# Weight pieces in two tiles that swap roles, and a queue that takes them step by step

## Chip, cores and metric

One core of a Trainium2 chip. The metric is the device time of one execution in microseconds (us); before the change it is 2639.64 us, the median of three runs (2638.79 to 2642.09).

## What is computed

One adaLN transformer block in float32: four batches of 512 tokens of width 1024; attention with 32 query heads in 8 groups that share a key and a value head, a causal window of 256 tokens; then eight LoRA experts. Cut to what matters here:

```python
q = rope(h @ wq); k = rope(h @ wk); v = h @ wv        # h: modulated layer norm of x
attn = softmax(where(allowed, q @ k.T * 128 ** -0.5, min))
out = (attn @ v).reshape(B, S, 4096) @ wo             # the wo product is the one concerned
x = x + ga * out
x = x + gb * lora_experts(h2)                         # h2: second layer norm
```

## The kernel before

**Numbers.** Every float32 operand of a matmul is split into a hi part (rounded to float32r) and a lo part (what is left); one product is three matmuls, hi by hi, lo by hi, hi by lo (`mm3`, lines 1123 to 1126).

**Groups.** The attention part runs over 32 groups n = 0 to 31: batch n // 8, head group n % 8. For each group TensorE projects K, Q0 to Q3 and V, runs 16 score tiles through softmax and the value product (`pe_attention`, steps u = 0 to 15), and multiplies by the group's 512 rows of wo (`pe_wo`, eight halves: four of them at the steps u = 8, 10, 12, 15, four behind the attention). In TensorE's order group n is: attention of n - 1 with the K projection of n inside it (`K_AT`; in the last group of a batch later, `K_LAST`, from step 5), the four last wo halves of n - 1, Q0 to Q3 of n, V of n.

**Batches.** Batch 0 loads the raw weights, splits them and stores the parts in DRAM (`w_d`). Batch 1 (groups 8 to 15) fetches the split parts. Batches 2 and 3 multiply by wo in a paired form with seven products for eight (`ORDER`, `OUTS`); five of its seven right sides (`MIXED`) are sums and differences of blocks of wo.

**Pieces.** These five are made on GpSimd during batch 1, in 28 pieces (`pool_mix`, line 1007). The queue (SyncE) loads two raw tiles (`sp_mix_load`, 751), GpSimd writes five sums to `mix_lo`, rounds them to `mix_hi` and puts sums less `mix_hi` into `mix_lo`; the queue stores both to `w_s` (`sp_mix_store`, 759). Before a piece GpSimd waits until both stores of the piece before have landed:

```python
            eng.wait_ge(s_raw, WS_KEPT + 32 * piece + 32)
            eng.wait_ge(s_mixd, WS_KEPT + 32 * piece)
```

`MIX_AT` (767) says which pieces belong to which group: 3 each in groups 8 to 12, 4 in 13 and 14, 2 in 15 and 3 in 16. GpSimd makes them behind its masked copies of the probabilities of the attention (`pool_fold`, line 1119) and ahead of the difference of values that the next attention needs (`pool_vd`, 1100).

**The queue's order** is written by hand and is strict: an instruction that waits holds all behind it. For a group of batch 1 (`sp_groups`, 779): the x tile and the turned x tile for the layer norm ahead (groups 9 to 12, `sp_turned_load`, 575; VectorE takes its statistics from the first at steps 11, 13 and 15 of the attention, line 1903), the Q and V weights (`sp_fetch_qv`, once V of the group before is done), K (`sp_fetch_ko`), then what `beside` says, then the wo weights once the group before has done its wo halves (`s_wo`, line 612), then the pieces that are left. `beside` holds the row of rstd and shift for the turned tile (`sp_turned_row`, 580; groups 9 to 12), up to three pieces, and the stores of the tile's two parts (`sp_tile_store`, 589). Behind group 15 `sp_reload` (627) loads hT of batch 2, which the K projection of group 16 reads during the attention of 15; then `sp_enter` (693) begins the paired stage, behind the last pieces.

Of the kernel before, what the change touches and what calls it, by code (L numbers as in the profile page):

```python
# [132 lines left out]
def adaln_block(nc, x, x_turned, wq, wk, wv, wo, gate_wT, lora_aT, lora_bT, c, wmod, cos, sin, mask, keep, lower, ident, iota, out):  # L133
# [12 lines left out]
    with ExitStack() as top:  # L146
# [631 lines left out]

        def sp_groups(eng, b, rows, store):
            if b < PAIRED:  # L780
                for g in range(1, KV):
# [3 lines left out]
                    def beside():
                        if g <= QT:
                            sp_turned_row(eng, b, t)
                        sp_mix(eng, g, range(2))
                        if g <= QT:
                            sp_tile_store(eng, b, t)  # L790
                        sp_mix(eng, g, range(2, min(3, MIX_AT[g + 1] - MIX_AT[g])))
# [2 lines left out]
                    sp_direct_group(eng, n, b, beside)
                    sp_mix(eng, g, range(3, MIX_AT[g + 1] - MIX_AT[g]))
                return
            if b == PAIRED:
                eng.wait_ge(s_mixd, WS_KEPT + 32 * PIECES * (KV - 1))
# [35 lines left out]
        def p1_sp(eng):  # L834
# [25 lines left out]

            def beside():
                sp_mix(eng, 0, range(2))
            sp_fetch_ko(eng, KV, 1, beside)
            sp_mix(eng, 0, range(2, 3))
# [1719 lines left out]
```

## Time and profile before

| | before |
|---|---|
| median of three runs | 2639.64 us |
| the profiled execution | 2638.18 us |
| its span | 2636.3 us |
| TensorE busy | 2520.9 us, 96% |
| VectorE, ScalarE, GpSimd busy | 67%, 44%, 39% |
| mean granted TensorE clock | 0.984 |
| chain that ended last | TensorE 72%, GpSimd 9%, DMA 8%, issue 4%, the queue 3% |

The span is what the profiler records from first to last instruction; the execution's own time is 1.9 us longer. A view of waits says which engine's instruction idled, for what, how often and how long. In a timeline, a bracket at the end of a row is the idle time ahead of it and what ended it. For a DMA a timeline shows when it was issued and how long the issue took, not when it landed.

### The profile page before, as it was taken

What the parts mean: (1) busy time and instruction counts of PE and PEld (TensorE: products, weight loads), DVE (VectorE), ACT (ScalarE), POOL (GpSimd) and SP (SyncE); (2) the same over time, 40 slices, a digit from 0 to 9 for tenths busy, and PEclk for the clock granted to TensorE, in tenths of its full rate; (3) what the DMA queues carried; (4) which work ended last, traced back from release to release, by engine and by line L of the source; (5) the groups of instructions that cost most, each with busy time, mean ns of one, the idle gap of its engine ahead of it and who ended that gap; (6) DMA issues with size and microseconds to landing.
All of it is one profiled execution on the core that took longest, in us unless ns stands there. A gap on an engine that the chain in (4) does not pass through costs nothing.

```text
span 2636.3 us, 42413 instructions
## 1 busy us (share of the span) xinstructions
PE 2520.9 (96%) x12281; PEld 2078.1 (79%) x12281; DVE 1773.3 (67%) x4798; ACT 1169.9 (44%) x2781; POOL 1023.8 (39%) x1278
## 2 busy tenths in 40 slices
PE   7999999999888988889989999999999999999999
PEld 4888888888666776777868888888888888887887
DVE  7677776667565655555677777777777777776653
ACT  4556654453243433333335555443444444445441
POOL 0332332334644544564464444331244443331122
PEclk9999999999899999999999999999999999999999
DMA  8766666676767566656687776666777777767321
GB/s 342 279 230 223 239 241 237 239 257 253 250 239 244 158 219 221 243 184 254 240 259 226 221 230 223 207 207 240 262 248 248 254 239 239 256 227 270 115 81 56
DMA packets 332543, 599.64 MB, mean 227 GB/s; under 512 B 20688, under 2 KB 211984, under 8 KB 330896
## 3 DMA queue, kind: packets, MB, share of 16 engines
q1 hardware_dynamic: 327968, 582.08, 63.3%
q10 hardware_dynamic: 4464, 16.25, 1.6%
q8 instruction: 48, 0.79, 0.1%
q14 instruction: 63, 0.52, 0.1%
HBM read 439.89 MB, written 158.38 MB: 227 GB/s over the span
## 4 chain that ended last, share of the span: by engine, by line
PE 72%; POOL 9%; DMA 8%; issue 4%; SPq 3%; DVE 2%; ACT 1%; DVEq 0%; POOLq 0%; ACTq 0%
PE bank L1124 22%; PE bank L1126 22%; PE bank L1125 22%; POOL mix_lo L1024 3%; PE bank L1288 3%; DMA w_o_lo<-w_o_lo_scratch 2%; POOL mix_hi L1020 2%; DMA w_s_lo_scratch<-mix_lo 2%; SPq L569 1%; DMA raw<-in_wo 1%; POOL mix_lo L1015 1%; POOL mix_lo L1017 1%; POOL mix_lo L1014 1%; POOL mix_lo L1013 1%; POOL mix_lo L1016 1%
## 5 line engine op out<-in xcount | busy, mean ns | idle before, releaser
L1471 ACT ACTIVATE prob<-prob,nbias 128x256 f32<-128x256 f32 (+1 forms) x512 | 247.1, 483 | 307.6 <-DVE nbias L1781 294.2
L1124 PE MATMUL bank<-hT_hi,w_q_hi 128*128 128x512 f32 x912 | 366.5, 402 | 6.7 <-DMA w_q_lo<-w_q_lo_scratch 6.7
L1124 PE MATMUL bank<-w_o_hi,qo_hi 128*128 128x512 f32 x744 | 303.4, 408 | 70.9 <-DMA w_o_lo<-w_o_lo_scratch 66.9
L1126 PE MATMUL bank<-hT_hi,w_q_lo 128*128 128x512 f32 x912 | 356.2, 391 | 0.0
L1125 PE MATMUL bank<-hT_lo,w_q_hi 128*128 128x512 f32 x912 | 355.9, 390 | 0.0
L1119 POOL TENSOR_TENSOR pT<-pT,lower_t 128x256 fp32r<-128x256 f32 x256 | 196.7, 768 | 362.1 <-DVE pT L1815 361.9
L1126 PE MATMUL bank<-w_o_hi,qo_lo 128*128 128x512 f32 x744 | 295.2, 397 | 0.0
L1125 PE MATMUL bank<-w_o_lo,qo_hi 128*128 128x512 f32 x744 | 294.8, 396 | 0.0
L1106 POOL TENSOR_TENSOR rotated<-v_all 128x256 f32<-128x256 f32 x64 | 47.7, 766 | 635.9 <-DVE v_all L1821 635.9
L1815 DVE TENSOR_TENSOR pT<-bank,pT 128x256 fp32r<-128x256 f32 (+1 forms) x512 | 196.1, 383 | 87.3 <-ACT pT L1603 86.8
L1603 ACT ACTIVATE pT<-bank 128x256 fp32r<-128x256 f32 (+1 forms) x512 | 178.5, 352 | 123.8 <-PE bank L1288 118.0
L1124 PEld LDWEIGHTS bank<-w_o_hi,qo_hi 128*128 128x128 f32 x744 | 143.0, 192 | 105.0 <-DMA w_o_lo<-w_o_lo_scratch 68.5
L1750 DVE TENSOR_TENSOR acc<-acc,bank 128x512 f32<-128x512 f32 x336 | 208.4, 682 | 17.8 <-PE bank L1126 15.9
L1710 DVE TENSOR_TENSOR rotated<-bank,cos_t 128x512 f32<-128x512 f32 x160 | 110.4, 690 | 149.4 <-ACT swapped L1454 149.2
L1465 ACT ACTIVATE qo_hi<-rotated 128x512 fp32r<-128x512 f32 x128 | 80.7, 631 | 281.9 <-DVE rotated L1714 281.9
L1124 PEld LDWEIGHTS bank<-hT_hi,w_q_hi 128*128 128x128 f32 x912 | 171.6, 188 | 40.0 <-DMA w_q_lo<-w_q_lo_scratch 6.9
L1126 PEld LDWEIGHTS bank<-hT_hi,w_q_lo 128*128 128x128 f32 x912 | 171.5, 188 | 36.4
L1125 PEld LDWEIGHTS bank<-hT_lo,w_q_hi 128*128 128x128 f32 x912 | 172.0, 189 | 30.8
L1288 PE MATMUL bank<-ident_t,prob 128*128 128x128 f32 x896 | 181.3, 275 | 13.5 <-DVE prob L1791 12.3
L1791 DVE TENSOR_SCALAR prob<-prob,rrow 128x256 f32<-128x256 f32 (+1 forms) x512 | 189.9, 376 | 0.0
L1781 DVE CUSTOM_DVE_ANT_0 prob<-bank,mask_t 128x256 f32<-128x256 f32 x384 | 162.2, 423 | 31.9 <-PE bank L1288 9.1
L1453 ACT ACTIVATE swapped<-bank 64x512 f32<-64x512 f32 x160 | 95.4, 596 | 184.6 <-PE bank L1126 172.4
(299 smaller groups left out, 6354.6 us busy)
## 6 DMA issues: line engine op xcount, KB each, us to landing
w_q_hi<-w_q_hi_scratch SPq DMA_DIRECT2D x82, 512.0 KB, 8.2
w_q_lo<-w_q_lo_scratch SPq DMA_DIRECT2D x82, 512.0 KB, 8.8
w_o_hi<-w_o_hi_scratch SPq DMA_DIRECT2D x68, 512.0 KB, 7.4
w_o_lo<-w_o_lo_scratch SPq DMA_DIRECT2D x68, 512.0 KB, 7.9
w_s_hi_scratch<-mix_hi SPq DMA_DIRECT2D x28, 640.0 KB, 3.7
w_s_lo_scratch<-mix_lo SPq DMA_DIRECT2D x28, 640.0 KB, 5.7
stage<-in_wq SPq DMA_DIRECT2D x32, 512.0 KB, 4.6
stage<-in_wo SPq DMA_DIRECT2D x32, 512.0 KB, 5.2
```

Source lines behind the costliest of these rows:

```text
L1119: eng.tensor_tensor(pair[:, :, 2, :], pair[:, :, 0, :].bitcast(F32), lower_t[:].unsqueeze(1).broadcast_to([P, 2, P]), ALU.mult).then_inc(s ...
L1124: eng.matmul(o, st[0], mv_[0], start=start, stop=False)
L1125: eng.matmul(o, st[0], mv_[1], start=False, stop=False)
L1126: return eng.matmul(o, st[1], mv_[0], start=False, stop=stop)
L1288: m = eng.transpose(bank[5 + u % 2][:, b * P:(b + 1) * P], prob[:, u % GQ, b * P:(b + 1) * P], ident_t[:])
L1471: eng.activation(tile, tile, ACT.Exp, bias=nbias[:, u:u + 1], scale=-1.0, accum_out=rowsum[:, u:u + 1]).then_inc(s_exp, 1)
L1603: eng.activation(pT[i % 2][0][:, 0:nk, h * P:(h + 1) * P], bank[5 + u % 2][:, 0:nk * P].rearrange("p (b q) -> p b q", q=P), ACT.Copy).then ...
L1710: eng.tensor_tensor(rotated[slot][:], bk[:], cos_t[:], ALU.mult).then_inc(s_dve, 1)
L1750: eng.tensor_tensor(a, a, M_BANK[p][i][:], ALU.add if sign > 0 else ALU.subtract).then_inc(s_wor, 1)
L1781: plain(eng.tensor_tensor_reduce(prob[:, u % GQ, 0:w], SBANK[u % 3][:, 0:w], add, -SCALE, FAR, ALU.add, ALU.min, nbias[:, u:u + 1])).then_ ...
L1791: plain(eng.tensor_scalar(tile, tile, rrow[:, u:u + 1], None, ALU.mult)).then_inc(s_nrm[u % GQ], 1)
L1815: eng.tensor_tensor(lo, bank[5 + u % 2][:, 0:nk * P].rearrange("p (b q) -> p b q", q=P), hi.bitcast(F32), ALU.subtract).then_inc(s_ptl, 1)
```

## The change

The tiles `mix_hi` and `mix_lo` become `mix[0]` and `mix[1]`. Piece p writes its sums to `mix[p % 2]`, rounds them to `mix[(p + 1) % 2]` and leaves the lo part in `mix[p % 2]`. The hi and the lo store have semaphores of their own (`s_mixh`, `s_mixd`). The sums of p wait for the hi store of p - 1, the rounding of p for its lo store. The hi store is issued as soon as the hi part is there.

In the queue, the steps of a piece (load the next raw tiles; store hi; store lo) stand one by one: for a group, the first piece's raw step and hi store, the turned row, its lo store, the second piece's raw step, then the wo weights, then all the rest of the pieces, and last the stores of the turned tile's parts. `MIX_AT` gives 4 pieces to group 15 (2 before) and 1 to group 16 (3 before). GpSimd's loop over groups 9 to 12 is written out. Where the paired stage waits for the stores it waits for both semaphores. The diff, cut:

```diff
-                mix_hi, mix_lo = split_pair(inner, "mix", [P, len(MIXED), 256])
+                mix = [sb(inner, f"mix{i}", [P, len(MIXED), 256], F32R) for i in range(2)]
...
-        MIX_AT = (0, 3, 6, 9, 12, 15, 19, 23, 25, 28)
-        def sp_mix(eng, g, pieces):
-            for i in pieces:
-                at = MIX_AT[g] + i
-                eng.wait_ge(s_mix, 3 * at + 1)
-                if at + 1 < MIX_AT[-1]:
-                    sp_mix_load(eng, divmod(at + 1, PIECES))
-                eng.wait_ge(s_mix, 3 * at + 3)
-                sp_mix_store(eng, divmod(at, PIECES))
+        MIX_AT = (0, 3, 6, 9, 12, 15, 19, 23, 27, 28)
+        def sp_mix_raw(eng, at):
+            eng.wait_ge(s_mix, 3 * at + 1)
+            if at + 1 < MIX_AT[-1]:
+                sp_mix_load(eng, divmod(at + 1, PIECES))
+        def sp_mix_hi(eng, at):
+            eng.wait_ge(s_mix, 3 * at + 2)
+            sp_mix_store(eng, at, 0).then_inc(s_mixh, 16)
+        def sp_mix_lo(eng, at):
+            eng.wait_ge(s_mix, 3 * at + 3)
+            sp_mix_store(eng, at, 1).then_inc(s_mixd, 16)
+        def sp_mix_piece(eng, at):
+            sp_mix_raw(eng, at)
+            sp_mix_hi(eng, at)
+            sp_mix_lo(eng, at)
+        def sp_mix_group(eng, n, b, g, row=lambda: None, store=lambda: None):
+            at, end = MIX_AT[g], MIX_AT[g + 1]
+            def before_o():
+                sp_mix_raw(eng, at)
+                sp_mix_hi(eng, at)
+                row()
+                sp_mix_lo(eng, at)
+                sp_mix_raw(eng, at + 1)
+            sp_fetch_ko(eng, n, b, before_o)
+            sp_mix_hi(eng, at + 1)
+            sp_mix_lo(eng, at + 1)
+            for i in range(at + 2, end):
+                sp_mix_piece(eng, i)
+            store()
...
-                    def beside():
-                        if g <= QT:
-                            sp_turned_row(eng, b, t)
-                        sp_mix(eng, g, range(2))
-                        if g <= QT:
-                            sp_tile_store(eng, b, t)
-                        sp_mix(eng, g, range(2, min(3, MIX_AT[g + 1] - MIX_AT[g])))
-                    sp_direct_group(eng, n, b, beside)
-                    sp_mix(eng, g, range(3, MIX_AT[g + 1] - MIX_AT[g]))
+                        sp_mix_group(eng, n, b, g, lambda: sp_turned_row(eng, b, t), lambda: sp_tile_store(eng, b, t))
...
-                sp_enter(eng, (b + 1) * KV, b + 1, (lambda: sp_mix(eng, KV, range(3))) if b < PAIRED else lambda: None)
+                sp_enter(eng, (b + 1) * KV, b + 1, (lambda: sp_mix_piece(eng, MIX_AT[KV])) if b + 1 == PAIRED else lambda: None)
...
         def pool_mix(eng, piece):
-            lo = mix_lo[:].bitcast(F32)
+            low, high = mix[piece % 2], mix[(piece + 1) % 2]
+            plain_sum = low[:].bitcast(F32)
             eng.wait_ge(s_raw, WS_KEPT + 32 * piece + 32)
-            eng.wait_ge(s_mixd, WS_KEPT + 32 * piece)
+            if piece:
+                eng.wait_ge(s_mix, 3 * piece)
+                eng.wait_ge(s_mixh, WS_KEPT + 32 + 16 * piece)
...
             eng.wait_ge(s_mix, 3 * piece + 1)
+            eng.wait_ge(s_mixd, WS_KEPT + 16 * piece)
             for i in range(len(MIXED)):
-                m = plain(eng.tensor_copy(mix_hi[:, i, :], lo[:, i, :]))
+                m = plain(eng.tensor_copy(high[:, i, :], plain_sum[:, i, :]))
```

How this moves instructions, at three places.

The queue, group 14, from the K weights of the next group on. Before:

```order
L569 DMA w_k_lo<-w_k_lo_scratch 128x1024
L757 DMA raw<-in_wo 128x2x256 x2
L765 DMA w_s_hi_scratch<-mix_hi 640x1x256
L765 DMA w_s_lo_scratch<-mix_lo 640x1x256
L757 DMA raw<-in_wo 128x2x256 x2
L765 DMA w_s_hi_scratch<-mix_hi 640x1x256
L765 DMA w_s_lo_scratch<-mix_lo 640x1x256
L757 DMA raw<-in_wo 128x2x256 x2
L765 DMA w_s_hi_scratch<-mix_hi 640x1x256
L765 DMA w_s_lo_scratch<-mix_lo 640x1x256
L569 DMA w_o_hi<-w_o_hi_scratch 128x1024
L569 DMA w_o_lo<-w_o_lo_scratch 128x1024
```

and now:

```order
L569 DMA w_k_lo<-w_k_lo_scratch 128x1024
L757 DMA raw<-in_wo 128x2x256 x2
L769 DMA w_s_hi_scratch<-mix 640x1x256
L769 DMA w_s_lo_scratch<-mix 640x1x256
L757 DMA raw<-in_wo 128x2x256 x2
L569 DMA w_o_hi<-w_o_hi_scratch 128x1024
L569 DMA w_o_lo<-w_o_lo_scratch 128x1024
L569 DMA w_o_hi<-w_o_hi_scratch 128x1024
```

Ahead of the wo weights stood three pieces' stores; now stand one piece's stores and two raw steps. The other stores follow behind the wo weights.

GpSimd, from the end of the first piece (s_ws7 is `s_raw`, s_ws8 `s_mixd`, s_ws9 `s_mixh`). Before:

```order
L1020 CAST mix_hi<-mix_lo 128x256 [waits s_mix,s_id]
L1020 CAST mix_hi<-mix_lo 128x256 [waits s_id] x4
L1024 TENSOR_TENSOR mix_lo<-mix_lo,mix_hi 128x256 [waits s_mix]
L1024 TENSOR_TENSOR mix_lo<-mix_lo,mix_hi 128x256 x4
L1013 TENSOR_TENSOR mix_lo<-raw 128x256 [waits s_ws8,s_ws7]
L1014 TENSOR_TENSOR mix_lo<-raw 128x256
L1015 TENSOR_TENSOR mix_lo<-raw 128x256
L1016 TENSOR_TENSOR mix_lo<-raw 128x256
L1017 TENSOR_TENSOR mix_lo<-raw 128x256
L1020 CAST mix_hi<-mix_lo 128x256 [waits s_mix,s_id]
L1020 CAST mix_hi<-mix_lo 128x256 [waits s_id] x4
```

and now:

```order
L1044 CAST mix<-mix 128x256 [waits s_ws8,s_mix,s_id]
L1044 CAST mix<-mix 128x256 [waits s_id] x4
L1048 TENSOR_TENSOR mix<-mix 128x256 [waits s_mix]
L1048 TENSOR_TENSOR mix<-mix 128x256 x4
L1036 TENSOR_TENSOR mix<-raw 128x256 [waits s_ws9,s_mix,s_ws7]
L1037 TENSOR_TENSOR mix<-raw 128x256
L1038 TENSOR_TENSOR mix<-raw 128x256
L1039 TENSOR_TENSOR mix<-raw 128x256
L1040 TENSOR_TENSOR mix<-raw 128x256
L1044 CAST mix<-mix 128x256 [waits s_ws8,s_mix,s_id]
L1044 CAST mix<-mix 128x256 [waits s_id] x4
```

The wait for the lo store has moved from the first sum to the rounding; the first sum waits for the raw tiles and the hi store.

The queue, end of group 15, up to the reload of hT (L636). Before:

```order
L765 DMA w_s_hi_scratch<-mix_hi 640x1x256
L765 DMA w_s_lo_scratch<-mix_lo 640x1x256
L569 DMA w_o_hi<-w_o_hi_scratch 128x1024
L569 DMA w_o_lo<-w_o_lo_scratch 128x1024
L569 DMA w_o_hi<-w_o_hi_scratch 128x1024
L569 DMA w_o_lo<-w_o_lo_scratch 128x1024
L569 DMA w_o_hi<-w_o_hi_scratch 128x1024
L569 DMA w_o_lo<-w_o_lo_scratch 128x1024
L569 DMA w_o_hi<-w_o_hi_scratch 128x1024
L569 DMA w_o_lo<-w_o_lo_scratch 128x1024
L636 DMA hT_hi<-hT_hi_scratch 128x1024
L636 DMA hT_lo<-hT_lo_scratch 128x1024
```

and now:

```order
L569 DMA w_o_hi<-w_o_hi_scratch 128x1024
L569 DMA w_o_lo<-w_o_lo_scratch 128x1024
L769 DMA w_s_hi_scratch<-mix 640x1x256
L769 DMA w_s_lo_scratch<-mix 640x1x256
L757 DMA raw<-in_wo 128x2x256 x2
L769 DMA w_s_hi_scratch<-mix 640x1x256
L769 DMA w_s_lo_scratch<-mix 640x1x256
L757 DMA raw<-in_wo 128x2x256 x2
L769 DMA w_s_hi_scratch<-mix 640x1x256
L769 DMA w_s_lo_scratch<-mix 640x1x256
L636 DMA hT_hi<-hT_hi_scratch 128x1024
L636 DMA hT_lo<-hT_lo_scratch 128x1024
```

The reload stood right behind the wo weights; now it stands behind the stores of three pieces.

## Rows read from the trace of the kernel before

**Rows 1.** The page, part 1: busy us (share of the span) xinstructions, TensorE.

```profile
PE 2520.9 (96%) x12281; PEld 2078.1 (79%) x12281; DVE 1773.3 (67%) x4798; ACT 1169.9 (44%) x2781; POOL 1023.8 (39%) x1278
```

**Rows 2.** The waits of TensorE: us in total, times, longest us.

```profile
PE bank L1124 <- DMA w_o_lo<-w_o_lo_scratch: 66.9, 7, 11.0
```

**Rows 3.** Windows; columns: us, busy of PE PEld DVE ACT POOL, PEclk, DMA share, GB/s.

```profile
756.00:760.00 4.00, 0.00 (x0) 0.00 (x0) 0.00 (x0) 0.00 (x0) 0.00 (x0) 0.50 1.03 419
760.00:764.00 4.00, 3.09 (x7) 2.48 (x8) 1.68 (x7) 0.26 (x1) 0.00 (x0) 0.50 1.02 409
764.00:768.00 4.00, 4.00 (x20) 3.37 (x19) 2.43 (x10) 1.43 (x6) 1.09 (x2) 0.92 1.03 411
```

**Rows 4.** Timeline of SyncE's queue, group 14: start us, us, what [idle].

```profile
1163.27 0.65 SPq L765 DMA_DIRECT2D w_s_lo_scratch<-mix_lo  x1
1163.96 1.35 SPq L569 DMA_DIRECT2D w_o_hi<-w_o_hi_scratch  x1
1170.42 0.65 SPq L569 DMA_DIRECT2D w_o_lo<-w_o_lo_scratch  x1
```

**Rows 5.** Timeline of GpSimd, group 14.

```profile
1118.52 0.73 POOL L1119 TENSOR_TENSOR pT<-pT,lower_t 128x256 fp32r<-128x256 f32 x1 [0.19 <-DVE pT L1815]
1125.72 3.98 POOL L1024 TENSOR_TENSOR mix_lo<-mix_lo,mix_hi 128x256 fp32r<-128x256 f32 x5
1135.36 0.73 POOL L1013 TENSOR_TENSOR mix_lo<-raw 128x256 f32<-128x256 f32 x1 [5.66 <-DMA w_s_lo_scratch<-mix_lo]
1178.24 1.40 POOL L1106 TENSOR_TENSOR rotated<-v_all 128x256 f32<-128x256 f32 x2
```

**Rows 6.** Timeline of TensorE, group 14: first Q matmul, first w_o matmul.

```profile
1132.11 0.39 PE L1124 MATMUL bank<-hT_hi,w_q_hi 128*128 128x512 f32 x1
...
1181.16 0.80 PE L1124 MATMUL bank<-w_o_hi,qo_hi 128*128 128x512 f32 x1 [7.51 <-DMA w_o_lo<-w_o_lo_scratch]
```

**Rows 7.** Tiles mix_hi and mix_lo: their stores.

```profile
DMA to landing us min/median/max: 3.6/3.7/6.9
...
DMA to landing us min/median/max: 4.9/5.7/8.5
```

**Rows 8.** Timelines of GpSimd, SyncE, TensorE and VectorE, groups 8 and 9.

```profile
633.83 5.79 POOL L1024 TENSOR_TENSOR mix_lo<-mix_lo,mix_hi 128x256 fp32r<-128x256 f32 x5
695.41 0.73 POOL L1119 TENSOR_TENSOR pT<-pT,lower_t 128x256 fp32r<-128x256 f32 x1 [0.19 <-DVE pT L1815]
...
673.26 1.36 SPq L577 DMA_DIRECT2D stage<-in_x  x1
...
673.65 0.80 PE L1124 MATMUL bank<-w_o_hi,qo_hi 128*128 128x512 f32 x1 [10.97 <-DMA w_o_lo<-w_o_lo_scratch]
...
680.13 0.69 DVE L1903 BATCH_NORM_STATS2 stats<-stage 128x6 f32<-128x512 f32 x1 [17.02 <-DMA stage<-in_x]
...
762.24 0.70 DVE L1903 BATCH_NORM_STATS2 stats<-stage 128x6 f32<-128x512 f32 x1 [9.81 <-DMA stage<-in_x]
```

**Rows 9.** Timelines of GpSimd, SyncE and TensorE, groups 15 and 16.

```profile
1200.24 0.73 POOL L1119 TENSOR_TENSOR pT<-pT,lower_t 128x256 fp32r<-128x256 f32 x1 [0.19 <-DVE pT L1815]
...
1239.40 0.43 SPq L636 DMA_DIRECT2D hT_lo<-hT_lo_scratch  x1
...
1248.67 0.47 PE L1124 MATMUL bank<-hT_hi,w_k_hi 128*128 128x512 f32 x1 [1.31 <-DMA hT_lo<-hT_lo_scratch]
```

**Rows 10.** Timelines of SyncE and TensorE, and a window, where batch 2 begins.

```profile
1327.56 0.65 SPq L765 DMA_DIRECT2D w_s_lo_scratch<-mix_lo  x1
...
1335.37 0.44 PE L1288 MATMUL bank<-ident_t,prob 128*128 128x128 f32 x2 [1.67 <-DVE prob L1791]
1342.48 0.79 PE L1124 MATMUL bank<-hT_hi,w_q_hi 128*128 128x512 f32 x1 [6.67 <-DMA w_q_lo<-w_q_lo_scratch]
...
1346.00:1348.00 2.00, 2.00 (x6) 1.52 (x6) 0.63 (x2) 0.00 (x0) 0.00 (x0) 0.50 1.04 414
```

**Rows 11.** Timeline of VectorE in group 10, after the turned tile.

```profile
801.12 0.69 DVE L1710 TENSOR_TENSOR rotated<-bank,cos_t 128x512 f32<-128x512 f32 x1 [3.53 <-ACT swapped L1454]
```

More of the change, by code:

```diff
@@ L516, in adaln_block @@
         s_so = s_ws[0:7]
-        s_raw, s_mixd = s_ws[7:9]
+        s_raw, s_mixd, s_mixh = s_ws[7:10]
         WS_KEPT = 32 * KV
@@ L757, in sp_mix_load, with mix_stored @@
                 eng.dma_start(raw[y][:], rows).then_inc(s_raw, 16)
-        def sp_mix_store(eng, piece):
-            g, jc = piece
-            j, half = divmod(jc, 2)
-            for z, tile in enumerate((mix_hi, mix_lo)):
-                to = w_s[z][bass.ds(g * P, P), :].rearrange("p (i j s n) -> p i j s n", i=len(MIXED), j=2, s=2)[:, :, j, half, :]
-                eng.dma_start(to, tile[:].bitcast(F32)).then_inc(s_mixd, 16)
-        MIX_AT = (0, 3, 6, 9, 12, 15, 19, 23, 25, 28)
-        def sp_mix(eng, g, pieces):
-            for i in pieces:
-                at = MIX_AT[g] + i
-                eng.wait_ge(s_mix, 3 * at + 1)
-                if at + 1 < MIX_AT[-1]:
-                    sp_mix_load(eng, divmod(at + 1, PIECES))
-                eng.wait_ge(s_mix, 3 * at + 3)
-                sp_mix_store(eng, divmod(at, PIECES))
+        def mix_stored(eng, pieces):
+            eng.wait_ge(s_mixh, WS_KEPT + 32 + 16 * pieces)
+            eng.wait_ge(s_mixd, WS_KEPT + 16 * pieces)
@@ new lines, in sp_mix_store @@
+        def sp_mix_store(eng, at, z):
+            g, jc = divmod(at, PIECES)
+            j, half = divmod(jc, 2)
+            to = w_s[z][bass.ds(g * P, P), :].rearrange("p (i j s n) -> p i j s n", i=len(MIXED), j=2, s=2)[:, :, j, half, :]
+            return eng.dma_start(to, mix[(at + 1 - z) % 2][:].bitcast(F32))
+        MIX_AT = (0, 3, 6, 9, 12, 15, 19, 23, 27, 28)
[3 more added lines that the diff above has]
+                sp_mix_load(eng, divmod(at + 1, PIECES))
@@ L783, in sp_groups @@
                     t = g - 1
[L785 to L791 removed]
                     if g <= QT:
                         sp_turned_load(eng, b, t)
[L794 to L795 removed]
+                        sp_fetch_qv(eng, n)
+                        sp_mix_group(eng, n, b, g, lambda: sp_turned_row(eng, b, t), lambda: sp_tile_store(eng, b, t))
+                    else:
+                        sp_fetch_qv(eng, n)
+                        sp_mix_group(eng, n, b, g)
                 return
             if b == PAIRED:
[L798 removed]
+                mix_stored(eng, MIX_AT[-1])
             for t in range(QT):
@@ L859, in p1_sp @@
             sp_mix_load(eng, (0, 0))
[L861 to L864, printed above, removed]
+            sp_mix_group(eng, KV, 1, 0)
             for b in range(1, last):
@@ L956, in p1_pool @@
             plain(eng.memset(acc[:], 0.0)).then_inc(s_acc0, 1)
-            with eng.Fori(1, 1 + QT) as g:
-                pool_group(eng, KV + g - 1)
-                for i in range(3):
-                    pool_mix(eng, 3 * g + i)
-            for g in range(1 + QT, KV + 1):
+            for g in range(1, KV + 1):
                 pool_group(eng, KV + g - 1)
@@ L1023, in pool_mix @@
             for i in range(len(MIXED)):
-                m = eng.tensor_tensor(mix_lo[:, i, :], lo[:, i, :], mix_hi[:, i, :].bitcast(F32), ALU.subtract)
+                m = eng.tensor_tensor(low[:, i, :], plain_sum[:, i, :], high[:, i, :].bitcast(F32), ALU.subtract)
             m.then_inc(s_mix, 1)
@@ L1579, in act_plain @@
             if i == 0:
-                eng.wait_ge(s_mixd, WS_KEPT + 32 * MIX_AT[-1])
+                mix_stored(eng, MIX_AT[-1])
             eng.wait_ge(s_pv, QT * n + i + 1)
```

12 lines of the change are left out of this document (6 added, 6 removed).

## The prediction

> **What bounds the kernel now.** TensorE is busy for 96% of the span [rows 1], so time can only be won where it idles or runs at the lower clock. The table of waits names one large item: seven waits of matmul line 1124 for w_o_lo, 66.9 us together [rows 2]. They lie in batch 1, one in each of groups 8 to 14. The windows around one of them show a second cost: the granted clock is 0.5 while TensorE idles and stays there after it resumes at 760.9 [rows 3], so each wait also slows what follows. I then followed the queue, GpSimd and TensorE through group 14. I call F the moment when GpSimd has done its last fold (1118.52 + 0.73 = 1119.25 there, [rows 5]) and count from it.
>
> - TensorE starts the Q projection at 1132.11, F+13 [rows 6]. The last matmul that reads w_o of the group before stands just ahead of it, so from F+13 on w_o may be overwritten.
> - The queue issues the w_o loads only at 1163.96, right behind the third piece's lo store at 1163.27 [rows 4]: F+45. The eighth load goes out at 1170.42 and has landed when TensorE resumes at 1181.16. TensorE wanted it 7.51 us earlier, at F+54.4 [rows 6].
> - GpSimd is why the third piece is so late: before each next piece it idles 5.66 us for the lo store [rows 5]. The store alone takes 4.9 us or more [rows 7].
>
> So the w_o loads are ready to go 32 us before they go, behind stores that nobody needs soon.
>
> **The change, part by part.**
>
> *1. The w_o loads move up.* Of the pieces, only the first one's stores and the second one's raw load stand ahead of them now. First piece: sums and hi part to F+6.4, lo part to F+10.5 (1125.72 and 3.98 us more, [rows 5]). The second piece's sums write the tile that held the first one's hi part; that store leaves at F+6.5 and takes 3.7 us [rows 7], so they start at about F+10.5, take 5 x 0.73 us [rows 5] and end at F+14.3. The raw load goes out, then w_o from F+15.6 to F+22.5 (eight issues in 7.1 us, [rows 4]). Landed 10 to 12 us later, by F+34, against a need at F+54.4: 20 us to spare. In groups 9 to 14 the wait is gone.
>
> *2. The clock.* TensorE resumes at 760.9; until 764 the clock is 0.50, and 0.92 from 764 to 768 [rows 3], which is 0.6 us more at half. 3.1 + 0.6 = 3.7 us at half speed cost 1.85 us a wait.
>
> Groups 9 to 14: 66.9 - 10.97 (group 8's, [rows 8]) = 55.9, and 6 x 1.85 = 11.1: **67.0 us**.
>
> *3. Group 8 is another case.* Its w_o comes in time too: the first piece's lo part ends at 639.6 [rows 8], w_o would be issued from about 645 to 652 (sums and a raw issue later) and land by 658 to 662, needed at 673.65 - 10.97 = 662.7. But VectorE has waited 17.02 us for stage<-in_x, until 680.13 [rows 8]; it stopped at 663.1, inside TensorE's own wait. That load is issued at 673.26 [rows 8], behind all pieces of group 8. What is late next is this load. After the change the stores of piece two are issued behind w_o, at 652, and land at about 660 to 662; piece three then takes to 669 or 670, and the load lands 6.9 us after its issue (673.26 to 680.13) at 676 or 677. VectorE starts 3 to 4 us earlier than now; with TensorE's small waits behind it I take **4 us** of the 12.8. Ends: 2 and 12.8 (10.97 and 1.85).
>
> *4. The same load in groups 9 to 11.* VectorE wants it at 762.24 - 9.81 = 752.4, and F there is 696.1 (695.41 + 0.73) [rows 8]: F+56.3. The second piece's stores now leave behind w_o at F+22.5; the hi store lands near F+30, so piece three runs from F+30 to F+41, then its store, the two hT stores that moved behind it, and the load at F+43. Landing at F+50: hidden, with 6 us of cover. Value: 0, which becomes a wait if that cover goes.
>
> *5. The row of the turned tile* now goes out behind the hi store and not ahead of it. The two small DMAs may come 2 to 3 us later. VectorE works on the tile and on one more sum, and then idles 3.53 us for ScalarE [rows 11]: 0, covered by that idle time.
>
> *6. Group 15 gets four pieces for two, and the hT reload stands behind them.* Piece by piece in a group without a turned tile: piece one ends at F+10.4, two at F+22, three at F+40.5 (held by the hi store behind w_o), four at F+52: its sums wait for the third hi store (F+40.5) and its hi part for the third lo store (F+45.3). The first hT pair is issued at F+52.7 to F+53.1. Now it is issued at 1239.40 and F is 1200.97, so F+38.4, and it lands after 9.3 us at 1248.67; TensorE wants it at 1248.67 - 1.31 = 1247.4, F+46.4 [rows 9]. With 6 to 7 us to land (6.9 in rows 8, fewer loads ahead) it comes at F+59.5: a wait of 13 us for 1.3, and up to 1.85 us at the low clock after it, as in part 2. **Loss 12.5 us.** Lower end: the stores pass w_o quickly, piece four ends at F+46, wait 6 us, loss 5. Upper end: landing after 9.3 us and the stores 3 us later, loss 18.
>
> The Trainium skill (page "DMA: Bandwidth & Descriptors", section "Anatomy of one DMA — SWDGE (gpsimd) path") fits a transfer as about 2.0 us plus bytes over 436 GB/s. By that the two hT loads of 1.05 MB would take an estimated 4.4 us and the loss would be 2 us smaller. The trace has 9.3 us for them and 6.9 us for the lone tile load, both with others in the queue; the measurement decides. (These loads are also issued from SyncE, and the page's fit is for GpSimd's path.)
>
> *7. Where batch 2 begins,* one piece is left for three. The last lo store is issued at 1327.56 [rows 10] and everything for the paired products stands behind it. TensorE idles 6.67 us for w_q_lo until 1342.48, after 1.67 us for VectorE at 1335.37; the clock is still 0.50 in the window 1346 to 1348 [rows 10]. From 1342.48 to 1348 at half speed costs 2.8 us. Two pieces less bring the last store forward by 20 us or more (a piece and its store are 16 us in [rows 5], 1118.52 + 0.73 to 1135.36), and 6.7 would hide the wait. **Gain 11 us** (6.67 + 2.8 + 1.67 of VectorE, on which ScalarE's work lies that waits for the last store by line 1580). Ends: 6.7, and 12.8 with a second such wait of VectorE.
>
> *8. GpSimd.* 28 pieces of fifteen operations as before; its loop over four groups is written out, which I cost at 0. It must be free for the v difference: now, in group 14, it starts that at 1178.24, F+59 [rows 5], later than it will (F+52).
>
> Sum: 67.0 + 4 - 12.5 + 11 = **69.5 us**. The profiled execution took 2638.18 us around its span of 2636.3; the median of the runs is 2639.64, 1.5 above it. 2638.2 - 69.5 = 2568.7, and on the median's scale **2570 us**.
>
> **The rivals.**
>
> *A. VectorE's tile load stays late in groups 9 to 11.* In favour: stores that stand behind 4.2 MB of w_o have no row of their own, and three transfers follow one another before the load. If each comes 10 us later than I take, the load misses F+56.3 by 5 to 8 us, three times, and group 15's hT by 5 more: 20 to 28 us given back, about 2593. Against: the cover of 6 us, and w_o itself lands within 11 us.
>
> *B. The queue passes stores and loads side by side.* Then piece three isn't held, hT waits only 5 or 6 us, and group 8 keeps 8 us of its wait: 2570 - 7 - 5 = 2558.
>
> *C. Slower: GpSimd takes the place of the queue.* Pieces three and four are held back by the hi store behind w_o until GpSimd is late for the v difference and the folds, and TensorE waits in the third value product. Place: the attention of each of groups 8 to 15. That product stands behind the first w_o matmul (step 13 against step 8), so it wants the difference after F+54.4; GpSimd needs some 3.5 us for it (1.40 for its first two operations, [rows 5]). It can decide once the pieces end after F+51 at the earliest, and it outweighs a saved wait of 9.3 us and 1.85 of clock only when they end after F+62, 10 to 20 us later than I work out. At 13 us lost in each of seven groups for 11.2 won, with hT 18, the time is 2638 + 13 + 18 - 11 + 1.5, about 2660. Against it: today, with every store waited for, they end at F+59.
>
> *D. The loads don't come earlier in fact,* because the queue still meets a wait ahead of them (the row of the turned tile, or the lo part of piece one): no change, 2640. Against: VectorE's row and piece one are ready by F+10.4 in [rows 5].
>
> **How the numbers follow.** My case 0.63, A 0.17, B 0.16, C 0.02, D 0.02. The forecast is 2570. My case with its bounds (group 8: 2 to 12.8, hT 5 to 18, batch 2: 6.7 to 12.8) reaches from 2560 to 2580; with B and A taken in, the range is 2554 to 2592. 0.2% (5 us) is about what a measurement of this kernel can tell from no change. Faster by more: 0.96 (my case, A and B); within: 0.02 (D); slower: 0.02 (C).
>
> **What would show it.** Right: no wait for w_o_lo in groups 9 to 14, and these groups 72 to 74 us apart; a VectorE wait for stage<-in_x of 10 us or more that is left in group 8 only; one wait of TensorE for hT_lo of 10 to 16 us in group 15's attention; none for w_q_lo where batch 2 begins. Wrong: VectorE waits for stage<-in_x in groups 9 to 11 (A); GpSimd idle under 2 us before piece three (B); TensorE waiting for vd or folds (C); w_o issued later than F+20 (D).

## The result, and the profile after

The changed kernel takes 2615.25 us (median of four runs, 2614.88 to 2617.47); the kernel before, run on the same chip beside it, 2640.86 us. The ratio is 0.9903, with a 95% interval of 0.9886 to 0.9921. It is faster, but by 25.6 us where 69.5 were forecast, and 2615 lies outside the range of 2554 to 2592. The profiled execution took 2614.88 us around a span of 2613.1. Every time and row below is of an undisturbed execution; experiment 2 had one more, of 13203 us, which its ratio leaves out.

TensorE's row of the page answers to [rows 1]:

```profile
PE 2518.0 (96%) x12281; PEld 2079.8 (80%) x12281; DVE 1771.3 (68%) x4798; ACT 1168.8 (45%) x2781; POOL 1013.4 (39%) x1278
```

The table of waits of the changed kernel (engine, line waited for: us in total, times, longest us), the rows that matter:

```profile
POOL mix L1036 <- DMA w_s_hi_scratch<-mix: 95.1, 10, 14.3
PE bank L1312 <- DVE prob L1815: 52.6, 15, 11.2
ACT prob L1495 <- DMA hT_lo_scratch<-l_lo: 49.4, 4, 14.5
DVE rrow L1810 <- ACT prob L1495: 38.5, 8, 12.0
PE bank L1148 <- DMA hT_lo<-hT_lo_scratch: 15.3, 1, 15.3
DVE stats L1927 <- DMA stage<-in_x: 13.9, 1, 13.9
```

(Line numbers are 24 higher here: 1148 is the matmul line 1124 of before, 1495 is ScalarE's exponential, 1312 the turn of the probabilities on TensorE.) The wait for w_o_lo, 66.9 us in [rows 2], has no row any more, and neither has w_q_lo, 6.7 us. In their place TensorE waits 52.6 us for `prob`. The kernel before has these two rows instead, and no wait of ScalarE for a hT store at all:

```profile
POOL mix_lo L1013 <- DMA w_s_lo_scratch<-mix_lo: 126.7, 19, 9.2
PE bank L1288 <- DVE prob L1791: 12.3, 15, 1.7
```

So the idle time of TensorE changed by -66.9 - 6.7 + 40.3 (prob) + 14.0 (hT_lo) = -19.3 us; of the other 4 of the 23.2 us that the span lost, 2.9 are busy time of TensorE (2520.9 to 2518.0 for the same matmuls: fewer of them ran at the lower clock, mean 0.986 after 0.984), the rest are small waits.

Where it happened can be read off one mark per group, the first matmul of the V projection. For groups 12, 13, 14 and 15 of the changed kernel:

```profile
985.60 0.45 PE L1148 MATMUL bank<-hT_hi,w_v_hi 128*128 128x512 f32 x1
1070.49 0.45 PE L1148 MATMUL bank<-hT_hi,w_v_hi 128*128 128x512 f32 x1
1141.69 0.45 PE L1148 MATMUL bank<-hT_hi,w_v_hi 128*128 128x512 f32 x1
1213.49 0.45 PE L1148 MATMUL bank<-hT_hi,w_v_hi 128*128 128x512 f32 x1
```

The same mark in both traces, as distances (us):

| from V of group to V of group | before | after | won | forecast |
|---|---|---|---|---|
| 8 to 9 | 88.1 | 87.5 | 0.6 | 4 |
| 9 to 13 (four groups) | 340.3 | 339.1 | 1.2 | 44.7 |
| 13 to 15 (two groups) | 164.1 | 143.0 | 21.1 | 22.3 |
| 15 to 16 | 77.4 | 92.0 | -14.6 | -12.5 |
| 16 to 17, batch 2 begins | 84.4 | 68.6 | 15.8 | 11 |

(44.7 and 22.3 are four and two sixths of the forecast's 67.0.) Four rows came as forecast within 5 us. Nearly the whole shortfall is in one: groups 9 to 12, the ones that carry a turned tile. There TensorE is idle for 41.2 us where it was for 44.4.

Group 10 shows how. F, GpSimd's last fold, is at 779.8 (a row at 779.06, 0.73 long). The queue in the changed kernel, from behind w_o to the x tile for group 11:

```profile
803.29 0.57 SPq L769 DMA_DIRECT2D w_s_hi_scratch<-mix  x1
804.84 2.38 SPq L769 DMA_DIRECT2D w_s_lo_scratch<-mix  x1
820.48 1.25 SPq L757 DMA_DIRECT2D raw<-in_wo  x2
822.84 0.56 SPq L769 DMA_DIRECT2D w_s_hi_scratch<-mix  x1
826.40 0.56 SPq L769 DMA_DIRECT2D w_s_lo_scratch<-mix  x1
827.01 0.65 SPq L592 DMA_DIRECT2D hT_hi_scratch<-l_hi  x1
827.70 1.39 SPq L592 DMA_DIRECT2D hT_lo_scratch<-l_lo  x1
829.12 1.56 SPq L577 DMA_DIRECT2D stage<-in_x  x1
```

and GpSimd, ScalarE, VectorE and TensorE in the same group:

```profile
816.03 0.74 POOL L1036 TENSOR_TENSOR mix<-raw 128x256 f32<-128x256 f32 x1 [11.22 <-DMA w_s_hi_scratch<-mix]
...
835.01 0.40 ACT L1495 ACTIVATE prob<-prob,nbias 128x128 f32<-128x128 f32 x1 [14.49 <-DMA hT_lo_scratch<-l_lo]
...
835.54 0.16 DVE L1810 RECIPROCAL rrow<-rowsum 128x1 f32<-128x1 f32 x1 [11.99 <-ACT prob L1495]
...
836.24 0.47 PE L1312 MATMUL bank<-ident_t,prob 128*128 128x128 f32 x1 [11.20 <-DVE prob L1815]
```

The third piece's sums are held until 816.03 by the hi store issued at 803.29. That piece's lo store leaves at 826.40, and only then the two stores of the turned tile. ScalarE has been idle since 835.01 - 14.49 = 820.5: its function for the projections ends with a wait for exactly these stores, before it goes on with the exponentials of the attention (`act_project`, here line 1538, line 1514 before):

```python
            if tile is not None:
                eng.wait_ge(s_hst, 32 * (tile + 1))
```

From there the lateness goes on to VectorE and to TensorE. In the kernel before, the same stores and ScalarE's first exponential behind its wait for them stand so (F is 781.0):

```profile
814.41 0.51 SPq L592 DMA_DIRECT2D hT_hi_scratch<-l_hi  x1
814.96 0.74 SPq L592 DMA_DIRECT2D hT_lo_scratch<-l_lo  x1
...
822.49 0.40 ACT L1471 ACTIVATE prob<-prob,nbias 128x128 f32<-128x128 f32 x1
```

The stores leave at F+33.4 before and at F+47.2 after. Before, the lo store landed 4.8 us after its issue, at 819.8; ScalarE was done with the projections at 822.35, F+41.4, and found it there. In the four groups the stores landed 2.4 to 3.0 us ahead of ScalarE. That was the whole cover, and the stores moved back by 14 us.

TensorE's waits for `prob` over 3 us are five: 10.97 in group 8 and 5.01, 11.20, 7.72 and 8.16 us (32.1 together) in groups 9 to 12. The one in group 8 has another cause: VectorE waits there for stage<-in_x, until 678.08.

### The profile page after: what moved, and what is told of

Same layout as the page of the kernel before. It is cut to its first block, busy times and chain, and to the rows that moved or that the text cites. A ratio compares the mean times of both kernels' runs of the same rounds, so it can differ in the third digit from the quotient of the medians.

```text
span 2613.1 us, 42328 instructions
## 1 busy us (share of the span) xinstructions
PE 2518.0 (96%) x12281; PEld 2079.8 (80%) x12281; DVE 1771.3 (68%) x4798; ACT 1168.8 (45%) x2781; POOL 1013.4 (39%) x1278
## 4 chain that ended last, share of the span: by engine, by line
PE 50%; DVE 1%; POOL 1%; DMA 1%; issue 0%; ACT 0%; ACTq 0%; SPq 0%; DVEq 0%; POOLq 0%
PE bank L1148 15%; PE bank L1150 15%; PE bank L1149 15%; PE bank L1312 2%; PE bank L2435 1%; PE bank L319 0%; DMA x1s<-x_scratch 0%; PE bank L1301 0%; DMA hT_lo<-hT_lo_scratch 0%; POOL mix L1048 0%; PE bank L1246 0%; DVE prob L1815 0%; PE bank L2486 0%; POOL mix L1044 0%; PE bank L2446 0%
## 5 line engine op out<-in xcount | busy, mean ns | idle before, releaser
L1312 PE MATMUL bank<-ident_t,prob 128*128 128x128 f32 x896 | 182.8, 276 | 53.9 <-DVE prob L1815 52.6
L1774 DVE TENSOR_TENSOR acc<-acc,bank 128x512 f32<-128x512 f32 x336 | 208.3, 680 | 17.7 <-PE bank L1150 15.8
L1312 PEld LDWEIGHTS bank<-ident_t,prob 128*128 128x128 f32 x896 | 122.0, 141 | 88.0 <-DVE prob L1815 65.9
L1148 PE MATMUL bank<-hT_hi,w_k_hi 128*128 128x512 f32 x368 | 167.3, 455 | 15.8 <-DMA hT_lo<-hT_lo_scratch 15.3
```

The lines of the kernel that those rows point to most:

```text
L1148: eng.matmul(o, st[0], mv_[0], start=start, stop=False)
L1312: m = eng.transpose(bank[5 + u % 2][:, b * P:(b + 1) * P], prob[:, u % GQ, b * P:(b + 1) * P], ident_t[:])
L1774: eng.tensor_tensor(a, a, M_BANK[p][i][:], ALU.add if sign > 0 else ALU.subtract).then_inc(s_wor, 1)
```

## The experiments

The theory after the result: *the time is lost by the tile stores' new place, through ScalarE's wait.* The rival: *it is lost by the pieces, GpSimd's longer hold behind w_o or the new order as such.* Times are medians; "before" is the kernel before, run beside them (2638.3 us, seven runs, for the first four; 2638.74 us, seven runs, for the next four).

**1. The tile stores ahead of the third piece** (label store_early), else the changed kernel:

```diff
             sp_mix_lo(eng, at + 1)
+            store()
             for i in range(at + 2, end):
                 sp_mix_piece(eng, i)
-            store()
```

> The changed kernel (2615.25 us, before 2640.86) with one move: the stores of the turned tile's two parts stand behind the second piece's lo store, ahead of the third piece, and not behind all pieces. Theory 1 (the gain was given back because ScalarE waits in line 1538 for these stores ahead of the next softmax, four times, 49.4 us, and TensorE then for prob): the stores land about 7 us after an issue at F+33.5, so near F+41, where ScalarE wants them (in group 10 it began to wait at F+40.8). The TensorE waits for prob of 5.0, 11.2, 7.7 and 8.2 us go, and 1.85 us of low clock with each: 32.1 + 7.4 = 39.5 us, the time is 2576 us (2570 to 2585). Theory 2 (VectorE has no time left to catch up once the w_o wait is gone, the stores only coincide): the waits for prob stay over 6 us each and the time stays over 2605.

Measured: 2573.61 us, ratio 0.9762 [0.9746, 0.9778]. Its waits:

```profile
POOL mix L1036 <- DMA w_s_hi_scratch<-mix: 100.7, 10, 14.8
PE bank L1312 <- DVE prob L1815: 21.4, 11, 11.8
PE bank L1148 <- DMA hT_lo<-hT_lo_scratch: 14.0, 1, 14.0
DVE stats L1927 <- DMA stage<-in_x: 14.7, 1, 14.7
```

ScalarE has no wait for hT_lo_scratch, and 41.6 us are back (37 by the two ratios, since the kernel before beside it was 2.6 us faster too), of the 43.9 that the gain fell short: the place of one line. The marks of V put it where the theory does: from group 9 to group 13 it takes 297.7 us, 41.4 less than in the changed kernel and 2 more than the forecast had. GpSimd is held behind w_o as much as in the change (100.7 us for 95.1), so that hold is not what cost the time. Theory held, the rival fell.

**2. The same move in the kernel before** (label before_store_late): its own order, but the tile stores behind all pieces and w_o:

```diff
                         sp_mix(eng, g, range(2))
-                        if g <= QT:
-                            sp_tile_store(eng, b, t)
                         sp_mix(eng, g, range(2, min(3, MIX_AT[g + 1] - MIX_AT[g])))
...
                     sp_mix(eng, g, range(3, MIX_AT[g + 1] - MIX_AT[g]))
+                    if g <= QT:
+                        sp_tile_store(eng, b, t)
```

> The kernel before with one move of the change alone: in groups 9 to 12 the stores of the turned tile's parts stand behind all pieces and the w_o loads, everything else is as before. Theory 1: ScalarE waits from F+41 until they land, near F+62 (issue at F+55 behind w_o), 20 us in each of four groups; TensorE's softmax step then comes so late that w_o has landed by then: 20 us in place of 9 to 10, four times, slower by 35 to 50 us, 2675 to 2690 us. Theory 2 (the stores only coincide): no change, 2641.

Measured: 2694.5 us, ratio 1.0214 [1.0197, 1.0232], 56 us slower than before, 4 to 20 more than expected. The trace is that of the same kernel run once more (label before_store_late_b):

> The kernel before with only the two stores of the turned tile moved behind all pieces of the group and behind the w_o loads, once more, for a usable trace; its time was 2694.5 us, 56 us above the kernel before. Theory: ScalarE's first exponential after the turned tile waits for the lo store of the tile, four times, 15 to 22 us each, and TensorE waits for prob in groups 9 to 12 about 10 to 14 us each, as in the changed kernel but longer, since the pieces end later. Rival (the late stores delay the w_o loads or the next tile load instead): no such wait of ScalarE, and TensorE's waits for w_o_lo or VectorE's for the tile have grown by 50 us.

Measured: 2695.67 us, and in the trace:

```profile
ACT prob L1471 <- DMA hT_lo_scratch<-l_lo: 101.0, 4, 26.8
PE bank L1288 <- DVE prob L1791: 97.4, 17, 24.0
PE bank L1124 <- DMA w_o_lo<-w_o_lo_scratch: 28.2, 3, 11.0
```

Four waits of ScalarE for `l_lo`, 101.0 us where there were none, and 85 us more of TensorE's waits for `prob`. The waits for w_o_lo fell from 66.9 to 28.2: w_o comes in time by itself when the attention is late for another reason. Hence 56 us and not 85: 85.1 - 38.7 = 46 us of waits more, and 10.4 us more of busy time (2531.3 for 2520.9) at a mean clock of 0.973 for 0.984. The mechanism is the same in both orders; the expected sizes of a wait (15 to 22 us for ScalarE, 10 to 14 for TensorE) were too small, and so was the range.

**3. The swap alone** (label swap_only): two tiles that change roles and stores with semaphores of their own, but the queue in its old order (up to three pieces, two in group 8, the tile stores behind the second, then w_o) and the old `MIX_AT`:

```diff
+            early = min(at + (2 if g == 0 else 3), end)
+
             def before_o():
-                sp_mix_raw(eng, at)
-                sp_mix_hi(eng, at)
                 row()
-                sp_mix_lo(eng, at)
-                sp_mix_raw(eng, at + 1)
+                sp_mix_piece(eng, at)
+                sp_mix_piece(eng, at + 1)
+                store()
+                for i in range(at + 2, early):
+                    sp_mix_piece(eng, i)
             sp_fetch_ko(eng, n, b, before_o)
-            sp_mix_hi(eng, at + 1)
-            sp_mix_lo(eng, at + 1)
-            for i in range(at + 2, end):
+            for i in range(early, end):
                 sp_mix_piece(eng, i)
-            store()
```

> The two tiles that swap roles, with separate hi and lo stores, but the queue's old order of duties (row, up to three pieces with the tile's stores behind the second, then w_o) and the old split of pieces (2 in group 15, 3 in group 16). Theory 1: GpSimd no longer idles 5.7 us before each piece, three pieces end near F+35 and w_o is issued at F+36, landed near F+54, where it is wanted at F+54.4: the w_o waits of groups 9 to 14 shrink to 0 to 3 us each, ScalarE doesn't wait for the stores, hT waits 1 to 2 us. Group 8 keeps about 9 us of its wait. 2641 - 67 + 0 to 15: 2575 to 2592, better than the changed kernel. Theory 2 (the swap brings little by itself, the order brings the gain): w_o waits stay over 5 us each and the time is over 2605.

Measured: 2567.06 us, ratio 0.9731 [0.9715, 0.9748], better than the lower end expected.

```profile
POOL mix L1036 <- DMA w_s_hi_scratch<-mix: 32.9, 8, 7.5
PE bank L1312 <- DVE prob L1815: 15.1, 16, 2.7
PE bank L1148 <- DMA w_o_lo<-w_o_lo_scratch: 11.5, 5, 3.1
```

GpSimd's waits for a store fall from 126.7 to 32.9 us, the three pieces end sooner, and in group 10 w_o leaves at F+40.3 (first issue at 808.01, F at 767.7) for F+47.4 before (828.36, F at 781.0). With these 7 us the wait for w_o_lo in that group falls from 9.96 to 1.62 us, and all of them from 66.9 to 11.5, though w_o leaves later than the F+36 expected. TensorE's busy time falls by 10.7 us with them (2510.2; mean clock 0.997). So the half of the change that I had priced as a side effect is worth 71 us alone, and the new order with the new split, which I had taken for the source of the gain, costs 45 to 48 us on top of it (by the ratios, or by the medians of the two sets of runs). What this run doesn't separate is the change of roles from the earlier hi store.

**4. The order alone** (label order_only): the changed queue and `MIX_AT`, but fixed roles, and the first sum of a piece waits for both stores:

```diff
-            return eng.dma_start(to, mix[(at + 1 - z) % 2][:].bitcast(F32))
+            return eng.dma_start(to, mix[1 - z][:].bitcast(F32))
...
-            low, high = mix[piece % 2], mix[(piece + 1) % 2]
+            low, high = mix[0], mix[1]
...
                 eng.wait_ge(s_mixh, WS_KEPT + 32 + 16 * piece)
+                eng.wait_ge(s_mixd, WS_KEPT + 16 * piece)
...
-            eng.wait_ge(s_mixd, WS_KEPT + 16 * piece)
```

> The changed kernel with the tiles' roles fixed as before (sums and lo in one, hi in the other; the first sum waits for the hi and the lo store of the piece before), in the new order with the new split. Theory 1: w_o still comes early (F+20 for F+16), no w_o waits; the pieces are some 4 to 6 us later each where they are not held by the hi store behind w_o, so ScalarE waits 1 to 6 us longer for the tile's stores in four groups and hT comes 4 to 8 us later: 2620 to 2645 us. Rival (the swap is of no use in this order, since the third piece is held by the store behind w_o either way): 2615 to 2620.

Measured: 2659.62 us, ratio 1.0081 [1.0064, 1.0097]: slower than before, above the 2645 expected.

```profile
POOL mix L1037 <- DMA w_s_lo_scratch<-mix: 174.8, 19, 15.9
PE bank L1312 <- DVE prob L1815: 87.3, 16, 18.4
ACT prob L1495 <- DMA hT_lo_scratch<-l_lo: 78.4, 4, 21.1
PE bank L1148 <- DMA hT_lo<-hT_lo_scratch: 24.6, 1, 24.6
```

The same two late things, each later: with fixed roles the pieces end later (the tile stores of group 10 leave at 847.60, F+53.8), and everything that stands behind the pieces follows. I had expected 1 to 6 us more for ScalarE in each of four groups and 4 to 8 more for hT; the rows show 7.3 a group (78.4 for 49.4) and 9.3 (24.6 for 15.3).

**5. The reload of hT ahead of group 15's fourth piece** (label reload_early), with the edit of experiment 1:

```diff
             for i in range(at + 2, end):
+                if i == end - 1:
+                    last()
                 sp_mix_piece(eng, i)
```

(`last` is `sp_reload(eng, b + 1)` in the last group of batch 1, and the reload behind the group is dropped there.)

> The changed kernel with two edits to the queue: the stores of the turned tile ahead of the third piece (alone: 2573.6 us) and, in group 15, the reload of hT ahead of the fourth piece. Theory (each late transfer is priced by its place in the queue): the wait of TensorE for hT_lo, 14.0 us in the run with the tile stores alone, falls to 0 to 3 us, with about 1.5 us of clock behind it; the last piece's stores go out a few us later, which the paired stage does not feel. 2558 to 2562 us. Rival (the two loads of hT are slow because of the 4.2 MB of w_o and the stores around them, wherever they stand): the wait stays at 8 us or more, 2566 to 2572.

Measured: 2567.46 us, ratio 0.9729 [0.9712, 0.9745], 6 us below experiment 1. The time lies in the range of the rival, but neither case came as it was put: the wait fell by half only, to 6.2 us, between the theory's 0 to 3 and the rival's 8. The first hT loads in the queue, and TensorE:

```profile
1185.62 0.58 SPq L636 DMA_DIRECT2D hT_hi<-hT_hi_scratch  x1
...
1194.08 0.77 PE L1151 MATMUL bank<-hT_hi,w_k_hi 128*128 128x512 f32 x1 [6.21 <-DMA hT_lo<-hT_lo_scratch]
```

In experiment 1 the first issue stands at 1190.41 and TensorE resumes at 1198.98 after 13.98 us. Against the moment at which TensorE wants hT (1187.9 here, 1185.0 there) the issue moved from 5.4 us behind to 2.3 us ahead, 7.7 us, and the wait fell by those 7.8. From first issue to TensorE it takes 8.5 us in both. The place in the queue sets the wait, as the theory says, and the loads are no faster in the new place, as the rival says. The theory's size was wrong: all 14 us were to go, but the fourth piece, which the loads passed, takes only 9.2 us in experiment 1 (from the third lo store at 1180.58 to the fourth at 1189.75), and the third piece, held behind w_o, still stands ahead.

**6. The old split of the pieces alone** (label pieces_old_split), else the changed kernel:

```diff
-        MIX_AT = (0, 3, 6, 9, 12, 15, 19, 23, 27, 28)
+        MIX_AT = (0, 3, 6, 9, 12, 15, 19, 23, 25, 28)
```

> The changed kernel with the old split alone: two pieces in group 15 and three in group 16; tile stores where the change put them. Theory: the wait for hT_lo (15.3 us) is gone down to 0 to 2 us; of the stall where batch 2 begins (9 to 11 us gained by the new split, as forecast) most comes back, or only 2 to 4 us, as in the kernel that has the swapped roles with the old queue order and the old split, where TensorE waits 1.3 us for w_q_lo with three pieces there. The waits for prob in groups 9 to 12 stay (ScalarE waits for the tile stores). 2600 to 2608 us. Rival (the split in itself is worth 11 us and hT only hides a wait that comes anyway): 2612 to 2618.

Measured: 2607.12 us, ratio 0.9883 [0.9867, 0.99], as the theory had it. TensorE has no wait for hT_lo, and none for w_q_lo either. ScalarE's row is as in the changed kernel:

```profile
ACT prob L1495 <- DMA hT_lo_scratch<-l_lo: 49.4, 4, 13.6
```

So the new split costs 8 us net (5 by the ratios, whose intervals overlap). The marks of V show both sides, with the old split first: 74.2 and 92.0 us from group 15 to 16, 78.0 and 68.6 from 16 to 17. The stretch with the wait for hT is 17.8 us longer with the new split, and the one where batch 2 begins 9.4 us shorter. Without it some stall is left there, not for w_q_lo but for `prob`:

```profile
1288.15:1366.13 77.98, 71.45 (x334) 58.43 (x333) 60.68 (x155) 36.24 (x95) 44.76 (x58) 0.98 0.77 250
```

(Columns as in [rows 3]: TensorE is busy for 71.45 of 77.98 us.)

**7. Two pieces ahead of w_o** (label two_ahead): experiment 3 with one number changed, so that two whole pieces and the tile stores stand ahead of w_o and the rest behind it:

```diff
-            early = min(at + (2 if g == 0 else 3), end)
+            early = at + 2
```

> Swapped roles and separate stores; in each group of batch 1 two whole pieces and the tile stores ahead of the w_o loads, all other pieces behind them; old split (two pieces in group 15, three in 16). Beside the kernel that has three pieces ahead (2567.1 us, TensorE waits 11.5 us for w_o_lo in five groups): w_o leaves 11 us earlier, so its waits vanish (11.5 us and 1 to 5 us of clock); the third piece is held behind w_o by 7 to 8 us a group, which delays the tile load of the next group by that; it has cover. Theory: 2556 to 2564 us. Rival (a third piece behind 4.2 MB of w_o costs through the tile load, VectorE's wait for the turned tile grows): 2565 to 2575.

Measured: 2557.79 us, ratio 0.9694 [0.9678, 0.971], in the theory's range and 9 us below experiment 3; TensorE waits for w_o_lo once, 2.5 us.

**8. And the first turned tile early** (label two_ahead_tile):

```diff
             sp_mix_load(eng, (0, 0))
+            sp_turned_load(eng, 1, 0)
             sp_mix_group(eng, KV, 1, 0)
...
                     if g <= QT:
-                        sp_turned_load(eng, b, t)
+                        if g > 1:
+                            sp_turned_load(eng, b, t)
                         sp_fetch_qv(eng, n)
```

> As the kernel with two pieces ahead of w_o, and the first turned tile of batch 1 (the load that group 9's place in the queue issues, behind all pieces of group 8) issued ahead of group 8's pieces. Theory: VectorE's wait of some 15 us for it, which sits on TensorE for about 11 us in group 8, is gone: 8 to 12 us faster than the kernel without this edit, 2546 to 2556 us. Rival (what follows group 8 is late anyway, for w_o or for another wait behind it): 0 to 3 us.

Measured: 2553.52 us (2553.28 to 2554.44), ratio 0.9678 [0.9661, 0.9694]; 4.3 us below experiment 7. The time is in the theory's range, the step is not: it lies between the two cases, and the intervals of the two ratios touch. Most of the stall of group 8 was gone already: in experiment 7 that load leaves at 664.20, not 672.95 as in the changed kernel, VectorE waits 7.19 us for it, and TensorE's longest wait in that group is 2.52 us. From V of group 8 to V of group 9 it takes 81.7 us there and 80.1 here. The page of this kernel and two rows of its waits:

```profile
PE 2507.6 (98%) x12281; PEld 2069.5 (81%) x12281; DVE 1777.0 (70%) x4798; ACT 1169.3 (46%) x2781; POOL 1032.0 (40%) x1278
```

```profile
POOL mix L1038 <- DMA w_s_hi_scratch<-mix: 48.8, 9, 9.2
PE bank L1314 <- DVE prob L1817: 13.2, 13, 2.4
```

This version beats both kernels: 85 us less than the kernel before, 62 less than the change (the latter across two sets of runs, whose kernels before differ by 2 us). It keeps the swap, drops the step-by-step order and puts the w_o loads, the tile stores and the first tile load where their readers need them. It is not the end: with the old split it takes 77.3 us from V of group 16 to V of group 17, where the changed kernel takes 68.6, and no run joins the new split to an hT reload that comes in time.

## Why the prediction was wrong

**The step that failed is part 4.** It moved "the two hT stores that moved behind it" as two items that stand ahead of VectorE's tile load, asked whether that load would still come in time, and valued the place at 0. The question that was not asked is who waits for the stores themselves. ScalarE does, in each of groups 9 to 12, between F+40.7 and F+42.1. Part 4's own working has them leave at about F+41, to land at F+46 to F+49: 5 to 8 us too late on my own numbers. The table of waits of before doesn't show this wait, since the stores landed 2 to 3 us before ScalarE came for them; it stood in the code only, as a `wait_ge` on the semaphore that the moved stores raise. Experiments 1 and 2 show it from both sides.

**A term in the same part was mis-sized.** "The hi store lands near F+30" was F+36: issued at 803.29 (F+23.5), it let the third piece start at 816.03 (F+36.2). The tile stores left at F+47.2, 6 us later than I worked out. So ScalarE waited 10.7 to 14.5 us a time, and not the 5 to 8 that my own numbers would have given.

Part by part:

- **Part 1** held: the first w_o load of group 10 leaves at 797.21, F+17.4 (forecast F+15.6), and no wait for w_o_lo is left. But in groups 9 to 12 the time went to `prob`.
- **Part 2** held where nothing took the wait's place: groups 13 and 14 gave 21.1 us for 22.3.
- **Part 3** was the right mechanism at the wrong end of its bounds. The load leaves at 672.95, not 669 to 670, and VectorE starts at 678.08, 2.05 us earlier, not 3 to 4; the group won 0.6 us, below the lower end of 2.
- **Part 5** held: VectorE waits 17.0 us in four times for the row where it waited 8.1, which is 2.2 us more a group (forecast 2 to 3), and TensorE feels little of it: groups 9 to 12 take 297.7 us in experiment 1 with 15.8 us of this wait, and 294.5 in experiment 7 with 6.5.
- **Part 6** held: first hT issue at 1232.56, F+54.1 (F is 1178.5), TensorE resumes at 1240.81, F+62.3, for F+59.5: a wait of 15.3 us for 13, a loss of 14.6 for 12.5. The two first hT loads took 8.2 us for the 6 to 7 that I took. The Trainium skill's fit ("DMA: Bandwidth & Descriptors", section "Anatomy of one DMA — SWDGE (gpsimd) path"), by which they would take an estimated 4.4 us, is not borne out by this trace, in which other transfers stand ahead of them.
- **Part 7** was the right stall, priced low: 15.8 us for 11, beyond the upper end of 12.8. The two windows below, of the kernel before and of the changed one, have the stretch from mark to mark (columns as in [rows 3]): for the same 333 matmuls TensorE's idle time went from 11.8 us to 0.1, and its busy time from 72.6 to 68.5. I had counted 8.3 us of idle time and 2.8 of clock. Left out were three short waits for `prob` (1.41 us at 1330.59, 0.24 at 1352.84, 1.11 at 1355.08) and 1.3 us of busy time. Experiment 6 shows that 9.4 us of this gain need the new split; the other 6.4 come without it.
- **Part 8** held: TensorE has no wait for the v difference.

```profile
1313.38:1397.78 84.40, 72.59 (x333) 59.09 (x333) 59.44 (x154) 35.90 (x95) 46.15 (x61) 0.94 0.75 242
...
1305.53:1374.11 68.58, 68.52 (x333) 57.45 (x333) 54.29 (x153) 36.38 (x95) 33.48 (x45) 1.00 0.75 234
```

**The rivals.** A was nearest in size (about 2593) and named late transfers behind w_o, which was half of it, but its victim, VectorE's tile load in groups 9 to 11, did not wait: that engine's only wait for stage<-in_x is 13.9 us in group 8, and 14.7 in experiment 1, where ScalarE no longer gives the load more time. B fell: GpSimd idles 11.22 us before piece three. C and D fell. The range left out a time that no case of mine gave, because all of them shared the blind spot of part 4. It was also narrower than its own parts: my case with every part at its end is 2552 to 2582, and not 2560 to 2580; 2615 lies outside that too.

**The signs.** No wait for w_o_lo, VectorE's wait in group 8 only, one wait for hT_lo of 10 to 16 us, none for w_q_lo: all these signs of being right came true, and the forecast was wrong all the same. Only one sign told: groups 9 to 14 were to lie 72 to 74 us apart, and 9 to 13 lie 84.8 apart (13 to 15: 71.5). Signs that name only the waits one knows of can't find the one that was overlooked; a distance can.

**What it got wrong about the whole.** I took the order for the source of the gain and the swap for a help to it. Experiments 3 and 4 show the reverse: the swap alone is worth 71 us, the order with its split alone costs 21. On top of the swap the order finds 11.5 us of w_o_lo waits to remove. It brings 37.5 us more of waits for `prob` (52.6 for 15.1), most of them behind the tile stores and the rest in group 8, and 15.3 for hT, with what the clock adds (busy time 2518.0 for 2510.2).

## What to carry to other kernels

When a transfer moves in a strict queue, ask two questions of it: what now stands behind it, and who waits for its landing; for a store that is the engine that reuses its source tile. A wait that the table doesn't show may be one that is met with 2 or 3 us to spare, so look in the code for every wait on the semaphore that a moved instruction raises, and compare its landing with the waiter's arrival. And if a queue is late because the producer ahead of it is slow, speed the producer up first: that alone may bring nearly everything behind it in time (71 us here), and then move only what is still late (9 us more in experiment 7).
